# Recommendation kernel on one core: top and dense layers over batches of up to four tiles, wider product rounds and chunks, and all engine programs unrolled, GpSimd's with new waits

## The chip, the cores and the metric

The kernel runs on one core of one Trainium2 chip. The metric is the device time of one execution in microseconds, as the median over runs. Three runs of the kernel before gave 768.77, 771.14 and 771.28 us; the median is 771.14 us.

## What is computed

The reference, cut to what matters (B = 2048 samples, 26 fields of 12500 rows, D = 64, all float32):

```python
emb = emb_tables[jnp.arange(26)[:, None], x_cat]          # 26 gathered rows a sample
dense_embed = price[:, None] @ Wp + bp                     # (B, 64)
feats = concat([transpose(emb, (1, 0, 2)), dense_embed[:, None, :]], axis=1)   # (B, 27, 64)
gram = einsum('bid,bjd->bij', feats, feats)                # 27 x 27 products a sample
interactions = gram[:, IU, JU]                             # the 351 pairs above the diagonal
h = relu(dense_embed @ W1 + b1)                            # 64 -> 128
dense_out = relu(h @ W2 + b2)                              # 128 -> 64
t = relu(concat([interactions, dense_out], axis=1) @ Wt1 + bt1)   # 415 -> 256
out = (t @ Wt2 + bt2)[:, 0]
```

## The kernel before

**Tiles.** The batch is cut into 16 tiles of 128 samples. For a tile, GpSimd issues one indirect DMA for each of the 26 fields (line 191); each fetches 128 rows of 64 floats, one row a partition, into `gathered`. That makes 416 gathers. They are grouped in four chunks of fields, (0, 8), (8, 16), (16, 24) and (24, 26), with one semaphore a chunk.

**Transposes.** When a chunk has landed, TensorE transposes two fields at a time (line 383), with 64 dimensions of two fields on 128 partitions. ScalarE copies the odd fields and VectorE the even ones out of PSUM into `feats` (line 139; line 154 for the last tile, whose samples are laid out differently so that half of the tile can be multiplied before all fields are there).

**Products.** A group is four samples; one matmul of a group against itself gives the 4 x 4 blocks of products of which the diagonal ones are wanted (line 414). A tile has 16 groups in each of two partition halves. They are done in four rounds of 32 samples, in two alternating PSUM buffers of two banks. After each round both engines copy the wanted blocks into `gram`, eight copies of 32 x 56 elements an engine (line 129).

**Dense and top layers.** In each tile, the dense branch takes two matmuls (lines 389 and 393) with ReLUs on ScalarE (lines 236 and 240), and the top layer takes for each half m of its 256 outputs one matmul with `dense_out` (line 425) and seven with `gram` (line 432). ScalarE and VectorE apply the ReLU (lines 245 and 336), a last product with `Wt2` gives the scores (line 440), and ScalarE stores them (line 249). An fp32 matmul of the program stands in the trace as two matmuls and two weight loads; a transpose as one of each.

**Order.** Each engine has its own program, and semaphores alone tie them. Four of them have a hardware loop: GpSimd over all 16 tiles, TensorE and ScalarE over tiles 1 to 13, VectorE over tiles 0 to 13, with the remaining tiles written out. In GpSimd's loop each chunk begins with a wait on `tile_idx_set[c]` (line 188) and a no-operation (line 189). `tile_idx` holds the row numbers of one tile alone: ScalarE refills a chunk's part of it from `row_idx` (line 219) once that chunk of the tile before has been transposed. So both the single `gathered` buffer and `tile_idx` come free by the same event. The tiles' row numbers are computed at the start by VectorE.

**The last tile.** Tile 15 is written out on TensorE: transposes of chunk 0 and the top layer of tile 14, transposes of chunk 1, scores of tile 14, dense branch, product rounds 0 and 1, transposes of chunks 2 and 3, rounds 2 and 3, top layer, scores. For tiles 14 and 15 `keep_warm` puts unused matmuls of 256 columns at set places (line 372): `WARM` gives their number, (0, 12, 4, 1, 1) for tile 14 and (0, 7, 3, 1, 1) for tile 15. SyncE writes the result at the end (line 167).

Of the kernel before, what the change touches and what calls it, by code (L numbers as in the profile page):

```python
# [6 lines left out]
FIELDS, VOCAB, BATCH, D = 26, 12500, 2048, 64  # L7
# [11 lines left out]
ROUNDS = 4  # L19
# [8 lines left out]
NPAIR = SLOTS * (SLOTS - 1) // 2  # L28

# [6 lines left out]
def rec_kernel(nc, price, x_cat, table, consts, w1, w2, wt1_pairs, wt1_dense, out):  # L36
# [3 lines left out]
    with ExitStack() as ctx:  # L40
# [25 lines left out]
        dense = sb("dense", [D, P])  # L66
        hidden = sb("hidden", [BM1, P])
        dense_out = sb("dense_out", [BM2, P])
        top = sb("top", [P, 2 * P])
# [11 lines left out]
        ps_top = [ps_mlp[m][:, 0:P] for m in range(2)]  # L81
        ps_hidden = ps_mlp[0][:, P:2 * P]
        ps_dense_out = ps_mlp[0][0:BM2, 2 * P:3 * P]
        ps_score = ps_mlp[1][0:1, P:2 * P]
# [12 lines left out]
        tile_idx_set = [sem(f"tile_idx_set{c}") for c in range(len(CHUNKS))]  # L97
        chunk_gathered = [sem(f"chunk_gathered{c}") for c in range(len(CHUNKS))]
        chunk_transposed = [sem(f"chunk_transposed{c}") for c in range(len(CHUNKS))]
# [18 lines left out]
        NC = len(CHUNKS)  # L118

        gram_to = gram[:, :].rearrange("p (j h g s) -> p h g j s", j=SLABS, h=2, g=GROUPS, s=GROUP)  # L120
        gram_from = [ps[:, :].rearrange("p (h g s j c) -> p h g s j c", h=2, g=RG, s=GROUP, j=PAD // GROUP, c=GROUP)
                     for ps in ps_gram]

        def evacuate_gram(copy, r, quads):

            last = None
            for s in quads:
                for c in range(GROUP):
                    last = copy(gram_to[QUAD * c:QUAD * (c + 1), :, RG * r:RG * (r + 1), :, s],  # L129
                                gram_from[r % 2][QUAD * s:QUAD * (s + 1), :, :, s, 0:SLABS, c])  # L130
            return last

        def evacuate_chunk(copy, c, q):
# [3 lines left out]
            src = ps_trans[c % 2][:, 0:n * P].rearrange("p (k h b) -> p h b k", k=n, h=2)  # L137
# [4 lines left out]
        def evacuate_unit_chunk(copy, c, kk):  # L142

            f0, f1 = CHUNKS[c]
            src = ps_trans[c % 2][:, :].rearrange("p (m q h b) -> p m q h b", m=BANK // P, q=2, h=2)
# [14 lines left out]
        def _(sp):  # L160
# [5 lines left out]
            sp.wait_ge(score_stored, TILES + 1)  # L166
# [4 lines left out]
        def _(pool):  # L171
# [13 lines left out]
            with pool.Fori(0, TILES) as t:  # L185
                for c, (f0, f1) in enumerate(CHUNKS):

                    pool.wait_ge(tile_idx_set[c], t + 1)
                    pool.nop(nofuse=True)  # L189
                    for f in range(f0, f1):  # L190
                        pool.indirect_dma_start(out=gathered[:, f * D:(f + 1) * D], out_offset=None, in_=rows,  # L191
                                                in_offset=bass.IndirectOffsetOnAxis(ap=tile_idx[:, f:f + 1], axis=0))\
                            .then_inc(chunk_gathered[c], 16)

        @block.scalar
        def _(act):
# [7 lines left out]
            act.wait_ge(rows_made, 3)  # L204
            act.sem_inc(trans_evac_act, 2)
            act.sem_inc(gram_evac_act, 2)
            act.sem_inc(score_stored, 1)

            def dense_features(dst, part, first, n, t):

# [321 lines left out]
```

## Time and profile before

| What | Value |
|---|---|
| median of three runs | 771.14 us (768.77 to 771.28) |
| profiled execution: span from its first to its last instruction | 540.9 us |
| profiled execution: its own time | not recorded apart from the span |
| median of the runs less the span | 230.2 us |
| GpSimd busy | 393.8 us, 73% of the span |
| TensorE matmuls busy | 291.1 us, 54% |
| ScalarE busy | 246.8 us, 46% |
| VectorE busy | 190.2 us, 35% |
| mean granted clock of TensorE | 0.719 |
| mean DMA rate | 30 GB/s |

The profile lists what lies between the first and the last instruction of the program. What the device does before and after, which the runs' times include, is in no row of it. A busy share is time with an instruction of that engine under way; only waits that end on the chain that finishes last are worth anything.

### The profile page before, as it was taken

What the parts mean: (1) busy time and instruction counts of PE and PEld (TensorE: products, weight loads), DVE (VectorE), ACT (ScalarE), POOL (GpSimd) and SP (SyncE); (2) the same over time, 40 slices, a digit from 0 to 9 for tenths busy, and PEclk for the clock granted to TensorE, in tenths of its full rate; (3) what the DMA queues carried; (4) which work ended last, traced back from release to release, by engine and by line L of the source; (5) the groups of instructions that cost most, each with busy time, mean ns of one, the idle gap of its engine ahead of it and who ended that gap; (6) DMA issues with size and microseconds to landing.
All of it is one profiled execution on the core that took longest, in us unless ns stands there. A gap on an engine that the chain in (4) does not pass through costs nothing.

```text
span 540.9 us, 6578 instructions
## 1 busy us (share of the span) xinstructions
PE 291.1 (54%) x1932; PEld 234.6 (43%) x1932; DVE 190.2 (35%) x672; ACT 246.8 (46%) x816; POOL 393.8 (73%) x425
## 2 busy tenths in 40 slices
PE   0027465382744638466382644727275372786785
PEld 0017354271533517255271533616154261574564
DVE  3016043160613416053160612516043160612553
ACT  0127255271734527265281733637255281733653
POOL 6777777777777777777777777777777777777750
PEclk9997758576585856667567685767758586588888
DMA  6333332333333333333333333333332333332110
GB/s 186 27 26 30 25 27 26 27 26 26 26 27 26 27 26 27 25 26 26 26 27 26 27 27 25 27 26 27 26 26 26 27 26 26 26 26 26 29 23 1
DMA packets 14345, 16.07 MB, mean 30 GB/s; under 512 B 7169, under 2 KB 7425, under 8 KB 14209
## 3 DMA queue, kind: packets, MB, share of 16 engines
q0 software_dynamic: 13312, 13.66, 31.2%
q1 hardware_dynamic: 578, 2.19, 1.1%
q10 hardware_dynamic: 448, 0.14, 0.1%
q8 instruction: 4, 0.07, 0.0%
q14 instruction: 3, 0.02, 0.0%
HBM read 15.95 MB, written 0.01 MB: 29 GB/s over the span
## 4 chain that ended last, share of the span: by engine, by line
POOL 70%; issue 26%; PE 1%; ACT 1%; DMA 1%; POOLq 1%; DVE 0%
POOL gathered L191 70%; PE ps_mlp L432 1%; ACT gram L129 1%; DMA gathered<-in_table,tile_idx 1%; DMA raw_idx<-in_x_cat 0%; POOLq L185 0%; PE ps_gram L414 0%; POOLq L40 0%; POOLq L189 0%; PE ps_mlp L425 0%; PE ps_mlp L440 0%; DVE feats L154 0%; DVE top L336 0%; ACT scores L249 0%; PE ps_trans L383 0%
## 5 line engine op out<-in xcount | busy, mean ns | idle before, releaser
L191 POOL DMA_INDIRECT gathered<-in_table,tile_idx x416 | 392.7, 944 | 128.6 <-issue 126.5
L383 PE MATMUL ps_trans<-ident,gathered 128*128 128x128 f32 x208 | 50.1, 370 | 189.9 <-DMA gathered<-in_table,tile_idx 189.0
L129 ACT COPY gram<-ps_gram 32x56 f32<-32x56 f32 x512 | 131.1, 256 | 41.9 <-PE ps_gram L414 35.2
L129 DVE COPY gram<-ps_gram 32x56 f32<-32x56 f32 x512 | 130.1, 254 | 54.4 <-PE ps_gram L414 46.6
L414 PE MATMUL ps_gram<-feats 64*128 64x128 f32 x1024 | 112.8, 395 | 38.1 <-ACT feats L139 18.2
L414 PEld LDWEIGHTS ps_gram<-feats 64*128 64x128 f32 x1024 | 102.4, 295 | 49.2 <-DVE gram L129 25.5
L139 DVE COPY feats<-ps_trans 64x256 f32<-64x256 f32 (+1 forms) x120 | 45.3, 378 | 218.4 <-PE ps_trans L383 217.2
L383 PEld LDWEIGHTS ps_trans<-ident,gathered 128*128 128x128 f32 x208 | 30.5, 180 | 205.8 <-issue 148.3
L219 ACT CAST tile_idx<-row_idx 128x8 uint32 (+3 forms) x61 | 12.0, 196 | 203.3 <-PE ps_trans L383 202.7
L432 PE MATMUL ps_mlp<-gram,wt1p_sb 128*128 128x128 f32 x448 | 69.6, 317 | 18.1 <-ACT gram L129 14.9
L432 PEld LDWEIGHTS ps_mlp<-gram,wt1p_sb 128*128 128x128 f32 x448 | 63.4, 225 | 24.1 <-DVE gram L129 21.5
L139 ACT COPY feats<-ps_trans 64x256 f32<-64x256 f32 (+1 forms) x120 | 53.8, 448 | 2.1
L336 DVE TENSOR_SCALAR top<-ps_mlp,consts_sb 128x128 f32<-128x128 f32 x16 | 5.6, 351 | 66.4 <-PE ps_mlp L432 66.4
L425 PE MATMUL ps_mlp<-dense_out,wt1d_sb 64*128 64x128 f32 x64 | 19.0, 383 | 0.0
L372 PE MATMUL ps_trans<-wt1p_sb,ident 128*128 128x256 f32 x60 | 16.1, 416 | 0.0
L245 ACT ACTIVATE top<-ps_mlp,consts_sb 128x128 f32<-128x128 f32 x16 | 5.9, 367 | 21.7 <-PE ps_mlp L432 21.7
L211 ACT ACTIVATE feats<-price_bc,consts_sb 64x64 f32 (+1 forms) x32 | 15.6, 487 | 0.4
L425 PEld LDWEIGHTS ps_mlp<-dense_out,wt1d_sb 64*128 64x128 f32 x64 | 11.9, 232 | 6.4 <-issue 5.2
L372 PEld LDWEIGHTS ps_trans<-wt1p_sb,ident 128*128 128x128 f32 x60 | 11.8, 207 | 2.4 <-issue 0.3
L440 PE MATMUL ps_mlp<-top,consts_sb 128*1 128x128 f32 x64 | 11.6, 314 | 0.4 <-DVE top L336 0.4
L393 PE MATMUL ps_mlp<-hidden,w_sb 128*64 128x128 f32 x32 | 11.0, 447 | 1.1 <-ACT hidden L236 1.1
L389 PE MATMUL ps_mlp<-dense,w_sb 64*128 64x128 f32 x32 | 9.6, 388 | 0.0
(26 smaller groups left out, 56.6 us busy)
## 6 DMA issues: line engine op xcount, KB each, us to landing
gathered<-in_table,tile_idx POOLq DMA_INDIRECT x416, 3.3
price_bc<-in_price SPq DMA_DIRECT2D x1, 1024.0 KB, 5.7
wt1p_sb<-in_wt_pairs SPq DMA_DIRECT2D x1, 896.0 KB, 8.3
raw_idx<-in_x_cat SPq DMA_DIRECT2D x1, 195.0 KB, 3.2
w_sb<-in_w ACTq DMA_DIRECT2D x2, 32.0 KB, 5.4
wt1d_sb<-in_wt_dense ACTq DMA_DIRECT2D x1, 64.0 KB, 8.2
consts_sb<-in_consts ACTq DMA_DIRECT2D x1, 4.5 KB, 2.0
raw_idx<-in_x_cat SPq DMA_DIRECT2D x1, 13.0 KB, 1.8
```

The lines of the kernel that those rows point to most:

```text
L129: last = copy(gram_to[QUAD * c:QUAD * (c + 1), :, RG * r:RG * (r + 1), :, s], gram_from[r % 2][QUAD * s:QUAD * (s + 1), :, :, s, 0:SLABS, c])
L139: last = copy(feats[D * h:D * (h + 1), :, 1 + f0 + q:f1 + q:2], src[D * q:D * (q + 1), h, :, :])
L191: pool.indirect_dma_start(out=gathered[:, f * D:(f + 1) * D], out_offset=None, in_=rows, in_offset=bass.IndirectOffsetOnAxis(ap=tile_idx[: ...
L211: return nc.scalar.activation(dst, price_bc[part, bass.ds(t * P + first, n)], ACT.Identity, bias=const(BP, part), scale=const(WP, part))
L219: nc.scalar.copy(tile_idx[:, f0:f1], row_idx[:, bass.ds((t + 1) * FIELDS + f0, f1 - f0)])\
L372: nc.tensor.matmul(ps_trans[bank][:, 0:TM1], ident[:, :], wt1p_sb[:, 0:TM1], start=True, stop=True)
L383: last = nc.tensor.transpose(ps_trans[c % 2][:, k * P:(k + 1) * P], gathered[:, f * D:(f + 2) * D], ident[:, :])
L393: nc.tensor.matmul(ps_dense_out, w2_sb[:, :], hidden[:, :], start=True, stop=True)\
L414: last = nc.tensor.matmul(ps_gram[r % 2][:, h * BANK + g * P:h * BANK + (g + 1) * P], group, group, start=True, stop=True)
L425: nc.tensor.matmul(ps_top[m], wt1d_sb[:, m * P:(m + 1) * P], dense_out[:, :], start=True, stop=False)
L432: last = nc.tensor.matmul(ps_top[m], wt1p_sb[:, j * TM1 + m * P:j * TM1 + (m + 1) * P], gram[:, j * P:(j + 1) * P], start=False, stop=(j = ...
L440: last = nc.tensor.matmul(ps_score, const(WT2 + m), top[:, m * P:(m + 1) * P], start=(m == 0), stop=(m == 1))
```

## The change

It does the following.

- **Chunks.** Tiles 0 to 14 have two chunks of fields, (0, 14) and (14, 26), in place of four. Their transposes go to one PSUM buffer of two banks. The last tile keeps the four chunks of before, in two alternating banks, under names of its own (`LAST_CHUNKS`, `last_gathered`, `last_transposed`).
- **Rounds.** Tiles 0 to 14 have two product rounds of 64 samples in place of four of 32. A round fills all four banks, so the next round waits until both engines have copied. Copies are of 32 x 112 elements, eight an engine and round. The last tile keeps four rounds in alternating buffers.
- **Batches.** The dense and top layers, the score product and their ReLUs run once for a batch of tiles: tiles 0-3, 4-7, 8-11, 12-13, 14 and 15, over up to 512 columns. `gram` holds two batches. The top layer of a batch stands on TensorE behind the first transposes of the next batch's first tile, its scores behind the second transposes. Hidden layer, dense output, top layer and scores share two PSUM banks; the hidden layer of a batch now waits for `score_stored` of the batch before.
- **GpSimd.** The loop over tiles is gone: 416 gathers are written out. `gathered` has two buffers. Row numbers are read straight from `row_idx`, now integers; `tile_idx`, ScalarE's refills of it (line 219) and the no-operation are gone. New waits: at each chunk, that the same chunk of the tile before has landed; at chunk 0 of tile t, that chunk 1 of tile t-2 has been transposed; at chunk 1 of tile t, that chunk 0 of tile t-1 has been. 
- **Loops.** TensorE, ScalarE and VectorE are written out too.
- **Warming.** The unused matmuls of tile 14 are gone; those of tile 15 stay as they were.

The diff, cut to its core:

```diff
-ROUNDS = 4
+ROUNDS = 2
-CHUNKS = [(0, 8), (8, 16), (16, 24), (24, 26)]
-WARM = {TILES - 2: (0, 12, 4, 1, 1), TILES - 1: (0, 7, 3, 1, 1)}
+CHUNKS = [(0, 14), (14, 26)]
+LAST_CHUNKS = [(0, 8), (8, 16), (16, 24), (24, 26)]
+LAST_ROUNDS = 4
+BATCHES = [(0, 4), (4, 8), (8, 12), (12, 14), (14, 15), (15, 16)]
+WIDE = 4
+BUFFERS = 2
+WARM = (0, 7, 3, 1, 1)
...
-        row_idx = sb("row_idx", [P, (TILES + 1) * FIELDS])
-        tile_idx = sb("tile_idx", [P, FIELDS], u32)
-        gathered = sb("gathered", [P, FIELDS * D])
+        row_idx = sb("row_idx", [P, TILES * FIELDS], u32)
+        gathered = sb("gathered", [P, BUFFERS * ROW])
-        gram = sb("gram", [P, SLABS * P])
+        gram = sb("gram", [P, 2 * SLABS * WIDE * P])
-        ps_gram = [pb(f"ps_gram{i}", [P, 2 * BANK]) for i in range(2)]
-        ps_trans = [pb(f"ps_trans{i}", [P, BANK]) for i in range(2)]
+        ps_gram = pb("ps_gram", [P, 4 * BANK])
+        ps_trans = pb("ps_trans", [P, 2 * BANK])
...
-            with pool.Fori(0, TILES) as t:
+            def gather(t, f, done):
+                at, to = t * FIELDS + f, (t % BUFFERS) * FIELDS + f
+                pool.indirect_dma_start(out=gathered[:, to * D:(to + 1) * D], out_offset=None, in_=rows,
+                                        in_offset=bass.IndirectOffsetOnAxis(ap=row_idx[:, at:at + 1], axis=0))\
+                    .then_inc(done, 16)
+
+            for t in range(LAST):
+                if t == 0:
+                    pool.wait_ge(rows_made, 1)
+                else:
+                    pool.wait_ge(rows_made, 3)
                 for c, (f0, f1) in enumerate(CHUNKS):
-
-                    pool.wait_ge(tile_idx_set[c], t + 1)
-                    pool.nop(nofuse=True)
+                    if t > 0:
+                        pool.wait_ge(chunk_gathered[c], 16 * (f1 - f0) * t)
+
+                    if c == 0 and t > 1:
+                        pool.wait_ge(chunk_transposed[1], t - 1)
+                    if c == 1 and t > 0:
+                        pool.wait_ge(chunk_transposed[0], t)
                     for f in range(f0, f1):
-                        pool.indirect_dma_start(out=gathered[:, f * D:(f + 1) * D], out_offset=None, in_=rows,
-                                                in_offset=bass.IndirectOffsetOnAxis(ap=tile_idx[:, f:f + 1], axis=0))\
-                            .then_inc(chunk_gathered[c], 16)
+                        gather(t, f, chunk_gathered[c])
+
+            pool.wait_ge(chunk_transposed[1], LAST - 1)
+            for c, (f0, f1) in enumerate(LAST_CHUNKS):
+                if c == 2:
+                    pool.wait_ge(chunk_transposed[0], LAST)
+                for f in range(f0, f1):
+                    gather(LAST, f, last_gathered[c])
...
-                if next_indices:
-                    nc.scalar.copy(tile_idx[:, f0:f1], row_idx[:, bass.ds((t + 1) * FIELDS + f0, f1 - f0)])\
-                        .then_inc(tile_idx_set[c], 1)
...
+            def hidden_layer(n):
+                pe.wait_ge(dense_made, n + 1)
+                if n > 0:
+                    pe.wait_ge(score_stored, n)
+                nc.tensor.matmul(ps_mlp[0][:, 0:width(n)], w1_sb[:, :], dense[:, 0:width(n)], start=True, stop=True)\
+                    .then_inc(hidden_summed, 1)
...
+            for t in range(LAST):
+                n = batch_of[t]
+                first = t == BATCHES[n][0]
+                transpose_chunk(t, 0)
+                if first and n > 0:
+                    top_layer(n - 1)
                 transpose_chunk(t, 1)
+                if first and n > 0:
+                    score(n - 1)
+                gram_round(t, 0)
+                if first:
+                    hidden_layer(n)
+                gram_round(t, 1)
+                if first:
+                    dense_out_layer(n)
+
+            n = batch_of[LAST]
+            transpose_last(0)
+            top_layer(n - 1)
+            transpose_last(1)
+            score(n - 1)
+            hidden_layer(n)
+            dense_out_layer(n)
+            for r in range(LAST_ROUNDS // 2):
+                gram_last(r)
+            transpose_last(2)
+            transpose_last(3)
+            for r in range(LAST_ROUNDS // 2, LAST_ROUNDS):
+                gram_last(r)
+            top_layer(n)
+            score(n)
```

On ScalarE the last tile's order becomes: copies of chunk 0, dense features, ReLU of the top layer of tile 14, copies of chunk 1, scores of tile 14, ReLU of the hidden layer, ReLU of the dense output, rounds 0 and 1. Before, the hidden ReLU and the dense output's stood ahead of the scores.

## Rows read from the trace of the kernel before

**Rows 1.** The page: span, and the chain that ended last, by engine
```profile
span 540.9 us, 6578 instructions
...
POOL 70%; issue 26%; PE 1%; ACT 1%; DMA 1%; POOLq 1%; DVE 0%
```

**Rows 2.** The gathers' line, whole span: duration min/median/max, idle before, time to landing
```profile
L191 POOL DMA_INDIRECT gathered<-in_table,tile_idx x416: 940/944/1114, 4.3 to 522.5; - x139
...
  issue: 126.5, 415
...
DMA to landing us min/median/max: 2.3/3.3/5.5
```

**Rows 3.** Timeline of GpSimd: gathers 0, 1, 26 and 415 (start us, us, what)
```profile
4.30 1.11 POOL L191 DMA_INDIRECT gathered<-in_table,tile_idx  x1 [2.16 <-DVE tile_idx L308]
5.71 0.94 POOL L191 DMA_INDIRECT gathered<-in_table,tile_idx  x1 [0.30 <-issue]
...
36.92 0.94 POOL L191 DMA_INDIRECT gathered<-in_table,tile_idx  x1 [0.30 <-issue]
...
522.47 0.94 POOL L191 DMA_INDIRECT gathered<-in_table,tile_idx  x1 [0.31 <-issue]
```

**Rows 4.** Busy time of two stretches (us, then PE, PEld, DVE, ACT, POOL; clock; DMA)
```profile
497.60:506.20 8.60, 6.13 (x55) 4.74 (x52) 8.11 (x32) 8.18 (x32) 6.51 (x7) 0.80 0.21 30
484.00:490.00 6.00, 3.94 (x19) 3.13 (x17) 0.00 (x0) 0.00 (x0) 4.49 (x5) 1.00 0.41 28
```

**Rows 5.** The gathers' line in 497 to 506 us, then in 484 to 490 us
```profile
L191 POOL DMA_INDIRECT gathered<-in_table,tile_idx x8: 940/944/947, 496.3 to 505.0; - x8
...
L191 POOL DMA_INDIRECT gathered<-in_table,tile_idx x5: 940/944/945, 483.8 to 488.8; - x5
```

**Rows 6.** The chain of waits from 505 us: GpSimd's sequencer at the loop's exit
```profile
508.59 1.09 POOLq L40
```

**Rows 7.** Groups of instructions by shape: busy us, mean ns | idle before
```profile
L129 DVE COPY gram<-ps_gram 32x56 f32<-32x56 f32 x512 | 130.1, 254 | 54.4 <-PE ps_gram L414 46.6
...
L139 DVE COPY feats<-ps_trans 64x256 f32<-64x256 f32 x90 | 37.6, 418 | 201.6 <-PE ps_trans L383 200.5
...
L139 DVE COPY feats<-ps_trans 64x64 f32<-64x64 f32 x30 | 7.7, 258 | 16.9 <-PE ps_trans L383 16.7
```

**Rows 8.** Timeline of the last tile's end, TensorE and ScalarE
```profile
513.46 0.60 PE L440 MATMUL ps_mlp<-top,consts_sb 128*1 128x128 f32 x4
...
515.12 0.37 ACT L236 ACTIVATE hidden<-ps_mlp,consts_sb 128x128 f32<-128x128 f32 x1
...
516.15 3.28 PE L414 MATMUL ps_gram<-feats 64*128 64x128 f32 x32
...
519.36 3.29 PE L372 MATMUL ps_trans<-wt1p_sb,ident 128*128 128x256 f32 x14
...
522.73 0.66 PE L383 MATMUL ps_trans<-ident,gathered 128*128 128x128 f32 x4
...
525.28 0.33 PE L383 MATMUL ps_trans<-ident,gathered 128*128 128x128 f32 x1 [0.60 <-DMA gathered<-in_table,tile_idx]
...
526.30 2.06 PE L414 MATMUL ps_gram<-feats 64*128 64x128 f32 x32 [0.25 <-DVE feats L154]
...
532.11 3.06 PE L432 MATMUL ps_mlp<-gram,wt1p_sb 128*128 128x128 f32 x14 [2.94 <-ACT gram L129]
...
535.83 1.83 PE L432 MATMUL ps_mlp<-gram,wt1p_sb 128*128 128x128 f32 x14
```

**Rows 9.** Busy time and granted clock of two stretches, columns as in rows 4
```profile
516.00:519.40 3.40, 3.40 (x35) 3.12 (x33) 1.06 (x5) 1.68 (x7) 2.56 (x3) 0.60 0.20 26
...
532.00:535.10 3.10, 2.99 (x14) 2.80 (x14) 0.00 (x0) 0.00 (x0) 0.00 (x0) 0.56 0.00 0
```

**Rows 10.** The page: DMA queues of kind instruction (packets, MB, share)
```profile
q8 instruction: 4, 0.07, 0.0%
q14 instruction: 3, 0.02, 0.0%
```

More of the change, by code:

```diff
@@ L203, in _, with dense_features @@
             act.wait_ge(feats_zeroed, 1)
[L204 to L209, printed above, removed]
-                return nc.scalar.activation(dst, price_bc[part, bass.ds(t * P + first, n)], ACT.Identity,
+            def dense_features(dst, part, first, n):
+                return nc.scalar.activation(dst, price_bc[part, first:first + n], ACT.Identity,
@@ L266, in _ @@
-            odd_fields(0, 0)
-            tile(0, first=True)
-            with act.Fori(1, TILES - 2) as t:
-                tile(t)
-            tile(TILES - 2, next_evacuate=evacuate_unit_chunk)
-            t = TILES - 1
-            dense_parts(t)
-            odd_fields(1, t, False, evacuate_unit_chunk)
-            hidden_relu(t)
-            dense_out_relu(t)
-            store_scores(t - 1)
-            for r in range(ROUNDS // 2):
+                evacuate_gram(nc.scalar.copy, t, r, (2, 3)).then_inc(gram_evac_act, 1)
@@ L342, in tile, with top_relu @@
+            def top_relu(n):
+                dve.wait_ge(top_summed[1], n + 1)
+                nc.vector.tensor_scalar(top[1][:, 0:width(n)], ps_mlp[1][:, 0:width(n)], const(BT1 + 1), 0.0,
+                                        ALU.add, ALU.max).then_inc(top_made, 1)
+            for t in range(LAST):
+                n = batch_of[t]
+                even_fields(0, t)
+                if t == BATCHES[n][0] and n > 0:
+                    top_relu(n - 1)
+                even_fields(1, t)
                 for r in range(ROUNDS):
@@ L343, in tile @@
                     gram_round(r, t)
[L344 to L354 removed]
+            t, n = LAST, batch_of[LAST]
+            even_last(0)
+            top_relu(n - 1)
+            even_last(1)
@@ new lines, in wait_trans_evac, with wait_gram_evac, transpose_fields @@
+            def wait_trans_evac(n):
+                if n > 0:
+                    pe.wait_ge(trans_evac_dve, n)
+                    pe.wait_ge(trans_evac_act, n)
+            def wait_gram_evac(n):
+                if n > 0:
+                    pe.wait_ge(gram_evac_dve, n)
+                    pe.wait_ge(gram_evac_act, n)
+            def transpose_fields(t, f0, f1, to):
+                base = (t % BUFFERS) * ROW
+                for k in range((f1 - f0) // 2):
+                    f = f0 + 2 * k
+                    last = nc.tensor.transpose(ps_trans[:, to + k * P:to + (k + 1) * P],
+                                               gathered[:, base + f * D:base + (f + 2) * D], ident[:, :])
+                return last
@@ new lines, in dense_out_layer, with gram_matmuls @@
+            def dense_out_layer(n):
+                pe.wait_ge(hidden_made, n + 1)
+                nc.tensor.matmul(ps_mlp[1][0:BM2, 0:width(n)], w2_sb[:, :], hidden[:, 0:width(n)], start=True, stop=True)\
+                    .then_inc(dense_out_summed, 1)
+            def gram_matmuls(first, groups, to, apart):
+                for g in range(groups):
+                    for h in range(2):
+                        at = (first + g) * GROUP
+                        group = feats[D * h:D * (h + 1), at:at + GROUP, :].rearrange("p s j -> p (s j)")
+                        out_at = to + h * apart + g * P
+                        last = nc.tensor.matmul(ps_gram[:, out_at:out_at + P], group, group, start=True, stop=True)
+                return last
@@ L473, in _ @@
-            score(t)
+            for t in range(LAST):
+                n = batch_of[t]
+                first = t == BATCHES[n][0]
+                transpose_chunk(t, 0)
+                if first and n > 0:
+                    top_layer(n - 1)
+                transpose_chunk(t, 1)
+                if first and n > 0:
+                    score(n - 1)
+                gram_round(t, 0)
+                if first:
+                    hidden_layer(n)
+                gram_round(t, 1)
+                if first:
+                    dense_out_layer(n)
```

304 lines of the change are left out of this document (136 added, 168 removed).

## Prediction

> **What bounds the kernel now.** I read the page's chain that ended last first, because it says whose time is the span. It names GpSimd for 70% and "issue" for 26%, every other engine for about 1% [rows 1]. Then the gathers' line: 416 of them, 0.944 us each with hardly any spread, and ahead of 415 of them an idle of 126.5 us in all, 0.305 us apiece, put down to "issue", that is, to nothing that the profile shows [rows 2]. The timeline confirms it: gather 1 starts at 5.71 us and gather 415 at 522.47 us, so the spacing is 516.76 / 414 = 1.248 us. Gather 26 is the first of tile 1, behind a pass of the loop, a wait and the no-operation, and has the same 0.30 us ahead of it as any other [rows 3]. So GpSimd never waits for another engine once it has begun. The span is: start until gather 0 at 4.30 us, the gathers until the last one's start at 522.47 us, and a tail of 540.9 - 522.5 = 18.4 us, in which the last fields land and the last tile is finished [rows 1, 3].
>
> Two further views say why the loop costs nothing. In the chain, GpSimd's sequencer is at the loop's exit at 508.59 us and done at 509.68 us, 12.8 us before the last gather starts [rows 6]: it runs some ten gathers ahead of the work. And where VectorE is busy 8.11 of 8.60 us the gathers take 940/944/947 ns, where it is idle 940/944/945 ns [rows 4, 5].
>
> The runs' median is 771.14 us, 230.2 us more than the profiled span; the profiled execution has no time of its own beside its span. These 230.2 us are in no row. I carry them over unchanged, and the doubt on them goes into the rivals.
>
> **The change, part by part.**
>
> GpSimd's program. 416 gathers stay, of the same shape: 128 rows of 64 floats by a column of 128 row numbers. Removed: 16 passes of the loop, 64 waits and 64 no-operations. They cost nothing now, because the sequencer does them about ten gathers ahead [rows 3, 6]. The spacing is bounded by 1.248 us (nothing changes) and 0.944 us (all "issue" gone, -126.5 us); the 0.305 us stand ahead of gathers with no wait, no loop and no no-operation between them as well as at the tile's border, so I take 1.248 us.
>
> The new waits. "Same chunk of the tile before has landed": at chunk 0 the last gather waited for started 13 gathers before, 16.2 us, against a landing of 3.3 us, at most 5.5 us [rows 2, 3]. At chunk 1 it is 15 gathers. While the sequencer waits, about ten gathers are queued. Cost 0. What stands behind such a wait on GpSimd is all later gathers, so these waits matter if they ever bite.
>
> The gates on the transposes. The nearest to biting is chunk 0 of tile t behind chunk 1 of tile t-2, where t-2 is first of a batch, since the wide top layer stands on TensorE ahead of that transpose. Its price: 14 matmuls of 128 columns took 1.83 us at full clock and 3.06 us at a granted clock of 0.56 [rows 8, 9]. For 512 columns I take between four times the one and four times the other, 7.3 to 12.2 us, twice for both halves, plus the products with `dense_out` at a seventh of that: 17 to 28 us. Chunk 1 lands 12 x 1.248 = 15.0 us behind chunk 0, so its transposes come 2 to 13 us late. The gate is looked at for a gather that starts 27 x 1.248 = 33.7 us after chunk 1's last gather, of which landing takes 3.3 us: 30 us of room against 13 us. Cost 0; the cover is gone only if the wide top layer takes over 45 us. At chunk 1 of tile t the gate asks for chunk 0 of tile t-1, which stands ahead of the top layer: no danger.
>
> TensorE, ScalarE and VectorE, tiles 0 to 14. Per tile two rounds of 32 matmuls, 2.06 to 3.28 us each [rows 8], each followed by eight copies of 112 elements. A copy of 56 took 254 ns, and 192 more elements a partition cost 418 - 258 = 160 ns on VectorE [rows 7], so I take 300 ns, between 254 (free) and 508 (double). A round is then 2.4 us of copies and a tile's rounds, no longer overlapped, 2 x (3.3 + 2.4) = 11.4 us at most, 15 us with the upper copy. With transposes and a quarter of a wide top layer it is under 30 us of a tile's 26 x 1.248 = 32.4 us. All of this gets cheaper for ScalarE and VectorE (fewer, larger copies, no refills) and hides behind the gathers before and after: worth 0.
>
> The start. One addition over 26 columns stands where four over 8, 8, 8 and 2 stood, and gather 0 waits for it and not for the first alone: some hundredths of a microsecond, and the no-operation is gone. 0.
>
> The tail. From the last landing on the program is the same: one transpose, 32 product matmuls, copies, 28 top matmuls, scores. What differs is what stands ahead. The hidden layer of tile 15 now waits for `score_stored` of tile 14. The score product ends at 514.1 us, but ScalarE stores scores behind the copies of chunk 1, which hold it until 515.1 us (the hidden ReLU started right then, at 515.12 [rows 8]). So scores are stored at about 515.5, the hidden matmuls run until 516.0, their ReLU until 516.5, the dense output's until 517.2, and rounds 0 and 1 start at 517.2 us where they started at 516.15: 1.0 us later. Behind them on TensorE stand 14 warming matmuls, which ended at 522.65, just ahead of the transposes of chunk 2 at 522.73 [rows 8]. These now start at 523.65. Then 0.66 us of transposes and six warming matmuls, 6/14 x 3.29 = 1.41 us, and chunk 3 can be transposed at 525.72 where it was at 525.28: **+0.4 us**. The lower end is -1.2 us, if the first 14 top matmuls meet full clock (3.06 down to 1.83). The upper end is +3.0 us: 0.4 and 1.2 for the products of rounds 2 and 3 (2.06 up to 3.28) and 1.2 for the second 14 top matmuls, with the remaining small ones in the rest. I take +0.4, since tile 15's order and its warming are unchanged.
>
> **Sum.** Span 540.9 + 0.4 = 541.3 us; with the 230.2 us outside, 771.5 us. A measurement of this kernel can tell about 0.3%, 2.3 us, from no change.
>
> **Rivals.**
>
> *Slower, the longer program.* Place: what is fetched and set up before the first gather, which no row shows, and the instruction queues. The trace has seven packets of 0.09 MB for them [rows 10]. By the code TensorE, ScalarE, VectorE and GpSimd hold about 1,400 instructions before (a quarter of what they execute) and 4,200 after, so 0.27 MB would move, 0.18 MB more. If that stands ahead of the work, at the gathers' rate of 26 to 28 GB/s, it is 7 us, **778 us**; the lower end is 0, if it is fetched beside the work. It decides from 2.3 us on, a third of it uncovered. For it: 230.2 us outside the span are unexplained. Against it: no engine in the span shows a stall for its instructions. 15%. The Trainium skill, Runtime: NRT & Kernel Launch, section Instruction fetch mechanics, says that a sequencer fetches the next block while it executes the present one, so that a long program is mostly hidden, and that a taken branch outside the fetched window stalls. By it the longer program costs nothing inside the span, which would leave the 771.5 us, and the trace agrees as far as the loop goes: 0.30 us at its border as elsewhere.
>
> *Slower, the clock in the tail.* The part before the last tile is less dense on TensorE (the warming of tile 14 is gone, the top layer is one block in four tiles). If all of the tail's matmuls run at the lower clock, it is the upper end, +3.0 us: **774.1 us**. For it: the clock was 0.60 in rounds 0 and 1 and 0.56 after the copies [rows 9]. Against it: tile 15's own warming is kept. 8%.
>
> *Slower, a gate that bites.* Four first tiles of batches with, say, 10 us each of stalled gathers. The room of 17 us above speaks against it: 3%, about 811 us.
>
> *Faster, the loop costs something where it is not profiled.* If the sequencer were not ahead in the timed runs, each of 16 passes would show what the exit took, 1.09 us [rows 6], and writing it out would give 17 us: **754 us**. The profiled execution shows the reverse, but cannot account for 230.2 us. 10%.
>
> *Faster, less contention.* If gathers were slowed by VectorE's traffic, halving its copies would shorten them; the most that the rows leave is 944 - 940 ns for 416 of them, 1.7 us: 769.8 us. Equal medians with VectorE busy and idle speak against it. 2%, counted as faster. The Trainium skill, GPSIMD Engine Reference, section Specifications, says that GpSimd shares its SBUF interfaces with VectorE and contends with some of its instructions. This trace shows no sign of it for these copies.
>
> **How the numbers follow.** The forecast case has 62%, of which 56 fall within 0.3% and 3 on either side, for the scatter of runs (768.77 to 771.28). Slower: 3 + 15 + 8 + 3 = 29%. Faster: 3 + 10 + 2 = 15%. Range: from 767 us, the lowest run less the tail's 1.2 and a little scatter, to 779 us, the longer program's 778 and scatter. It leaves out the unprofiled loop and the biting gate, 13%, and some edges.
>
> **What would show it.** In the changed kernel's profile: gathers at 0.94 us with 0.30 us ahead of each, first start near 4.3 and last near 522.5 us; no wait of GpSimd on TensorE; the wide top layer 17 to 28 us and its tile's second transposes late by 2 to 13 us; rounds 0 and 1 of tile 15 about 1 us later, the last transpose at 525.7; a span of 541.3 us. I am wrong if the spacing of gathers moves, if gathers wait for transposes, or if median and span no longer stand 230 us apart: the last would say that the program's length or its loops cost time that the profile doesn't cover.

## The result and the profile after

The kernel after took 675.37 us (median of four runs, 673.98 to 683.1), beside 769.95 us for the kernel before in the same session: a ratio of 0.8795 with a 95% interval of 0.8748 to 0.8842, 12% faster. I had predicted 771.5 us and no change.

The first thing to read is that in each of these runs the recorded span is 1.8 us short of the time: 673.98 us stand beside a span of 672.2 us. In every timed execution of this study that has both, whatever the kernel, they are 1.75 to 2.11 us apart. The 230.2 us "outside the span" of the prediction therefore never lay outside. They were the difference between two conditions in which a chip can be. The trace with a span of 540.9 us [rows 1] was of the one, the 771 us of the other. I call them **quiet** (the kernel before takes 543 to 544 us) and **disturbed** (763 to 770 us). Of the chips used below, 2, 3, 6 and 9 were quiet. Chip 14 was disturbed, in both series of runs made on it, and is the only such chip here; which chips the runs of this section used is not on record. For reading a change, each condition needs a trace of its own.

The page of the kernel after, taken in the disturbed condition (span; busy time of each engine; the chain that ended last, by engine; the instruction queues):

```profile
span 672.2 us, 4362 instructions
...
PE 256.0 (38%) x1496; PEld 180.9 (27%) x1496; DVE 145.4 (22%) x358; ACT 169.1 (25%) x405; POOL 393.8 (59%) x425
...
q8 instruction: 12, 0.20, 0.1%
...
q14 instruction: 10, 0.08, 0.0%
...
another core or an unknown queue 51%; issue 15%; DVE 13%; PE 13%; ACT 7%; DMA 0%; SPq 0%; ACTq 0%
```

No engine is busy for 60% of the span, GpSimd has left the chain [rows 1 had it at 70%], and half of it is put down to "another core or an unknown queue" in a program on one core. That name, "remote" in other views, is given to a wait that no recent event in the trace explains. The gathers' line and the longest waits of the same kernel (us in total, times, longest):

```profile
L200 POOL DMA_INDIRECT gathered<-in_table,row_idx x416: 938/944/1112, 3.7 to 623.7; - x139
...
  issue: 121.3, 398
  PE ps_trans L421: 97.8, 15
...
  remote: 9.3, 2
```

```profile
DVE gram L141 <- remote: 330.0, 24, 55.2
ACT gram L141 <- remote: 324.9, 24, 55.3
...
POOL gathered L200 <- PE ps_trans L421: 97.8, 15, 20.6
```

Duration and issue gap of a gather are those of [rows 2]; new are 107.1 us (97.8 and the 9.3 under "remote") in which GpSimd stands still for transposes, about once a tile. The timeline of the kernel after shows what is late (start us, us, what, idle before it):

```profile
41.43 3.79 PE L458 MATMUL ps_gram<-feats 64*128 64x128 f32 x32 [1.30 <-issue]
...
45.00 1.52 PE L443 MATMUL ps_mlp<-dense,w_sb 64*128 64x512 f32 x2
...
96.53 3.17 ACT L141 COPY gram<-ps_gram 32x112 f32<-32x112 f32 x8 [55.34 <-remote]
...
99.95 3.79 PE L458 MATMUL ps_gram<-feats 64*128 64x128 f32 x32 [53.43 <-ACT gram L141]
...
106.59 0.94 POOL L200 DMA_INDIRECT gathered<-in_table,row_idx  x1 [20.62 <-PE ps_trans L421]
```

The product round ends at 45.22 us, and the copies that read it start at 96.53 us, 51 us later. Nothing else held ScalarE or VectorE. The semaphore events kept in the trace say that it is the signal that is late and not the copies: the increment behind this round stands at 96.51 us, and at 45.25 us, 0.03 us behind the round's last matmul, in the quiet trace of the same kernel that is read further down. The windows view tells when they were let go (window, length, then for PE, PEld, DVE, ACT and POOL the busy time with its instructions, granted clock, DMA share, GB/s):

```profile
46.50:86.00 39.50, 0.02 (x1) 0.00 (x0) 0.00 (x0) 0.00 (x0) 30.03 (x32) 0.54 0.33 27
86.00:96.50 10.50, 0.00 (x0) 0.00 (x0) 0.00 (x0) 0.00 (x0) 0.00 (x0) 0.50 0.04 3
96.50:106.00 9.50, 5.87 (x41) 4.55 (x41) 5.23 (x14) 5.94 (x15) 0.00 (x0) 0.60 0.00 0
```

For 39.5 us GpSimd gathers, and the other engines stand still with finished products in PSUM. Then the gate stops GpSimd, and 10.5 us into that pause everything goes on at once.

### The profile page after: what moved, and what is told of

Read it like the earlier page. It is cut to its first block, busy times and chain, and to the rows that moved or that the text cites. A ratio compares the mean times of both kernels' runs of the same rounds, so it can differ in the third digit from the quotient of the medians.

```text
span 672.2 us, 4362 instructions
## 1 busy us (share of the span) xinstructions
PE 256.0 (38%) x1496; PEld 180.9 (27%) x1496; DVE 145.4 (22%) x358; ACT 169.1 (25%) x405; POOL 393.8 (59%) x425
## 4 chain that ended last, share of the span: by engine, by line
another core or an unknown queue 51%; issue 15%; DVE 13%; PE 13%; ACT 7%; DMA 0%; SPq 0%; ACTq 0%
DVE gram L141 9%; PE ps_mlp L489 8%; ACT gram L141 5%; DVE feats L151 3%; PE ps_gram L458 2%; ACT feats L151 1%; PE ps_trans L421 1%; PE ps_trans L404 1%; PE ps_mlp L481 1%; DVE top L370 0%; ACT feats L239 0%; DMA raw_idx<-in_x_cat 0%; DVE feats L352 0%; ACT feats L166 0%
## 5 line engine op out<-in xcount | busy, mean ns | idle before, releaser
L200 POOL DMA_INDIRECT gathered<-in_table,row_idx x416 | 392.6, 944 | 229.9 <-issue 121.3
L141 ACT COPY gram<-ps_gram 32x112 f32<-32x112 f32 (+1 forms) x272 | 97.1, 357 | 395.5 <-remote 324.9
L141 DVE COPY gram<-ps_gram 32x112 f32<-32x112 f32 (+1 forms) x272 | 96.6, 355 | 404.3 <-remote 330.0
L489 PE MATMUL ps_mlp<-gram,wt1p_sb 128*128 128x512 f32 (+2 forms) x168 | 63.0, 538 | 7.5 <-DVE gram L141 4.2
L151 DVE COPY feats<-ps_trans 64x448 f32<-64x448 f32 (+1 forms) x60 | 36.7, 612 | 50.4 <-issue 40.8
L151 ACT COPY feats<-ps_trans 64x448 f32<-64x448 f32 (+1 forms) x60 | 34.1, 569 | 44.3 <-PE ps_trans L421 24.1
L489 PEld LDWEIGHTS ps_mlp<-gram,wt1p_sb 128*128 128x128 f32 x168 | 33.6, 234 | 39.2 <-issue 24.7
L239 ACT ACTIVATE feats<-price_bc,consts_sb 64x64 f32<-64x64 f32 x32 | 15.7, 490 | 0.7
L481 PE MATMUL ps_mlp<-dense_out,wt1d_sb 64*128 64x512 f32 (+2 forms) x24 | 13.5, 655 | 4.0 <-ACT dense_out L271 2.6
L404 PE MATMUL ps_trans<-wt1p_sb,ident 128*128 128x256 f32 x24 | 6.1, 391 | 0.0
```

The lines of the kernel that those rows point to most:

```text
L141: last = copy(gram_to[QUAD * c:QUAD * (c + 1), n % 2, t - BATCHES[n][0], :, rg * r:rg * (r + 1), :, s], source[QUAD * s:QUAD * (s + 1), :, ...
L151: last = copy(feats[D * h:D * (h + 1), :, 1 + f0 + q:f1 + q:2], src[D * q:D * (q + 1), h, :, :])
L200: pool.indirect_dma_start(out=gathered[:, to * D:(to + 1) * D], out_offset=None, in_=rows, in_offset=bass.IndirectOffsetOnAxis(ap=row_idx[ ...
L239: return nc.scalar.activation(dst, price_bc[part, first:first + n], ACT.Identity, bias=const(BP, part), scale=const(WP, part))
L404: nc.tensor.matmul(ps_trans[:, BANK * bank:BANK * bank + TM1], ident[:, :], wt1p_sb[:, 0:TM1], start=True, stop=True)
L481: nc.tensor.matmul(ps_mlp[m][:, 0:w], wt1d_sb[:, m * P:(m + 1) * P], dense_out[:, 0:w], start=True, stop=False)
```

## The experiments

The working theory, R in what follows: in the disturbed condition, **while gathers stream, what TensorE has finished is made known to the other engines only slowly, and the lag is worked off when the gathers pause.** In the expectations, A1 is the form of it in which the gates' pauses help, and A2 the rival in which they are pure loss. C is a second rival, without any lag: the chain of transposes, copies and products itself is slow, and instructions beside it are free.

**The kernel before, unchanged** (chip 14). 

> The kernel before, unchanged, to see what a profiled execution of it looks like beside its timed ones. Theory A (the execution whose trace was shown first was an unusual one; the timed ones contain stalls such as the changed kernel's trace shows, in which products are done and the copies that wait for them start tens of us later): span about 768 us, GpSimd's gathers interrupted by waits of some 230 us in all. Theory B (230 us lie outside the span of every execution): span 541 us again and a time of 770 us.

764.42 us, ratio 1.0002; profiled span 761.8 us. This is the trace that the prediction should have had:

```profile
span 761.8 us, 6578 instructions
```

```profile
L191 POOL DMA_INDIRECT gathered<-in_table,tile_idx x416: 938/944/1479, 4.3 to 726.0; - x139
...
  ACT tile_idx L219: 206.2, 15
  issue: 123.5, 400
```

```profile
41.07 3.79 PE L414 MATMUL ps_gram<-feats 64*128 64x128 f32 x32 [1.10 <-issue]
...
76.03 8.86 ACT L129 COPY gram<-ps_gram 32x56 f32<-32x56 f32 x32 [35.27 <-remote]
...
85.88 0.94 POOL L191 DMA_INDIRECT gathered<-in_table,tile_idx  x1 [16.47 <-ACT tile_idx L219]
```

GpSimd stands still for 206.2 us, in 15 of 16 tiles. The account of the 89.6 us between the two spans: pauses 206.2 - 107.1 = 99.1 us less, issue gaps 2.2 less, start 0.6 less, which puts the last gather 102 us earlier; the tail behind it grows from 35.8 to 48.5 us, 12.7 more.

**Without gates** (chip 14).

```diff
-BUFFERS = 2
+BUFFERS = 16
-                    if c == 0 and t > 1:
-                        pool.wait_ge(chunk_transposed[1], t - 1)
-                    if c == 1 and t > 0:
-                        pool.wait_ge(chunk_transposed[0], t)
```

> The changed kernel with 16 buffers for the gathered rows and no wait of GpSimd on transposes. Theory A1 (the stalls end when the gates stop the gathers, so the stream of gathers itself holds up the semaphores of TensorE): gathers without a pause until about 523 us, one long stall of TensorE until then, and after it the work of up to 15 tiles at about 20 us each, 750 to 850 us. Theory A2 (the stalls have another cause and the gates only hand them on to GpSimd): gathers end at 523 us, TensorE is at most one stall behind, 545 to 600 us.

873.84 us, 1.1455 (1.1348 to 1.1563): the slowest of all, and above the 750 to 850 us of A1. The gathers run through without a pause, 3.8 to 557.3 us, and the span is 868.5 us. Its gathers' line, and stretches of its timeline:

```profile
L200 POOL DMA_INDIRECT gathered<-in_table,row_idx x416: 940/947/1799, 3.8 to 557.3; - x139
```

```profile
118.80 3.14 ACT L141 COPY gram<-ps_gram 32x112 f32<-32x112 f32 x8 [77.54 <-remote]
...
122.19 3.75 PE L451 MATMUL ps_gram<-feats 64*128 64x128 f32 x31 [75.22 <-issue]
...
139.78 0.37 PE L414 MATMUL ps_trans<-ident,gathered 128*128 128x128 f32 x1 [2.43 <-issue]
...
141.18 0.18 PEld L414 LDWEIGHTS ps_trans<-ident,gathered 128*128 128x128 f32 x1 [2.62 <-issue]
...
142.58 0.37 PE L414 MATMUL ps_trans<-ident,gathered 128*128 128x128 f32 x1 [2.43 <-issue]
...
143.98 0.18 PEld L414 LDWEIGHTS ps_trans<-ident,gathered 128*128 128x128 f32 x1 [2.62 <-issue]
...
435.20 3.06 DVE L141 COPY gram<-ps_gram 32x112 f32<-32x112 f32 x8 [86.47 <-remote]
...
454.80 1.28 DVE L151 COPY feats<-ps_trans 64x448 f32<-64x448 f32 x2 [16.54 <-remote]
...
471.60 1.21 DVE L151 COPY feats<-ps_trans 64x384 f32<-64x384 f32 x2 [15.52 <-remote]
...
561.20 3.13 DVE L141 COPY gram<-ps_gram 32x112 f32<-32x112 f32 x8 [88.39 <-remote]
```

Weight loads and matmuls alternate at exactly 1.40 us, with nothing that they wait for. The last four lines show the same beat in the signals. VectorE's copies start 19.6, 16.8 and 89.6 us apart, which is 14, 12 and 64 times 1.40 us, and 14, 12 and 64 are the numbers of TensorE instructions between them: seven transposes, six transposes and a product round, with their weight loads. So while gathers stream, the lag is counted in instructions, one per 1.40 us, and not in the time that they take.

In the other direction nothing is slow here: ScalarE's copies end at 121.94 us and TensorE starts its round at 122.19. A2 falls. Without pauses TensorE does, at 1.40 us each, some 395 instructions in the 553 us of the gathers (the trace has 408 started by then), two tiles of 16 and a part of the third, and the rest afterwards, in 311 us.

The gathers themselves also take longer in places, which neither form expected: they end at 557.3 us and not at 523, and GpSimd is busy 427.5 us against 393.8. From 220 us on, 163 of them follow each other at 1.40 us as well. What the two have in common is not shown.

**One part alone** (chip 14): only GpSimd written out, with direct row numbers and the gate on the transposes in place of ScalarE's refill; then only the other three loops written out.

```diff
-            with pool.Fori(0, TILES) as t:
+            for t in range(TILES):
-                    pool.wait_ge(tile_idx_set[c], t + 1)
-                    pool.nop(nofuse=True)
+                    pool.wait_ge(rows_made, 1 if t == 0 else 3)
+                    if t > 0:
+                        pool.wait_ge(chunk_transposed[c], t)
```

> The kernel before with GpSimd's program alone written out: row numbers read from row_idx, at each chunk one wait that the same chunk of the tile before has been transposed, no refills by ScalarE. If GpSimd's loop or its refilled row numbers cost the time (the rival in which the loop costs something in the timed runs): 545 to 680 us. If the chunks, rounds and batches did it: 770 us as before.

```diff
-            with act.Fori(1, TILES - 2) as t:
+            for t in range(1, TILES - 2):
-            with dve.Fori(0, TILES - 2) as t:
+            for t in range(0, TILES - 2):
-            with pe.Fori(1, TILES - 2) as t:
+            for t in range(1, TILES - 2):
```

> The kernel before with the loops of TensorE, ScalarE and VectorE written out and GpSimd's loop kept. If waits against register values and loop passes on these three engines cost the time: 545 to 680 us. If a longer program costs time: over 775 us. If neither: 770 us.

GpSimd's part: 716.06 us from two runs 2.6% apart (706.72, 725.4), so 38 to 57 us less than the 763.49 us beside it, with no interval; in the trace of the 725.4 us run GpSimd's pauses are 169.5 us, for 206.2. It takes away a loop and a hop over ScalarE, whose refill stands behind that engine's other work; which of the two counts was not separated. The three loops: 747.53 us, 0.9799 (0.9677 to 0.9922), a gain that may be under 1%. Both times lie between the values expected, so neither part alone is the whole cause. A program written out is not slower, against the rival of the longer program.

**More for TensorE, fewer passes for TensorE, more pauses.** Each was run on a quiet and on the disturbed chip. The first expectation of each pair had the disturbed condition in mind and met quiet chip 6, where it doesn't apply.

```diff
+                for _ in range(32):
+                    nc.tensor.transpose(ps_trans[:, 2 * BANK - P:2 * BANK], ident[:, :], ident[:, :])
                 gram_round(t, 1)
```

> The changed kernel with 32 unused transposes of the identity more on TensorE in each of tiles 0 to 14, between the two product rounds (64 matmuls and weight loads a tile, about 2 us of TensorE, which is busy 38%). Theory R (while gathers stream, TensorE gets rid of finished instructions, and with them of its semaphore increments, at only one in about 1.4 us; only in pauses of the gathers does it catch up, at some 16 in a microsecond by 187 instructions a tile and 10 us lost a tile): 64 more cost about 4 us a tile, 675 + 60 = 735 us. Theory C (the chain of transposes, copies, products and copies is what is late, and instructions beside it are free): at most 2 us a tile on that chain, 675 to 705 us.

> The changed kernel with 32 unused transposes more on TensorE in each of tiles 0 to 14. Where the kernel before takes 544 us they cost nothing (542.9 us). Theory R where it takes 765 us: about 4 us a tile, 735 us, a ratio of 0.96. Theory C: 675 to 690 us, a ratio of 0.88 to 0.90.

```diff
-        feats = sb("feats", [P, HALF, PAD])
+        feats = sb("feats", [P, HALF, PAD], mybir.dt.bfloat16)
```

> The changed kernel with feats held in bfloat16, so that a product is one matmul and one weight load in place of two and two: 64 instructions a tile fewer on TensorE. The products are rounded to bfloat16 inputs. Theory R: about 4 us a tile less, 675 - 60 = 615 us. Theory C: products take half of 3.8 us a round, 7 us a tile less of a chain that waits for nothing else, 570 us if that chain set the time, or no change if the stalls are of another kind.

> The changed kernel with feats in bfloat16, 64 instructions a tile fewer on TensorE, inputs of the products rounded. Where the kernel before takes 544 us it changes nothing (543.6 us). Theory R where it takes 765 us: about 615 us, a ratio of 0.80. If the number of instructions on TensorE doesn't matter: 675 us, 0.88.

```diff
                     for f in range(f0, f1):
                         gather(t, f, chunk_gathered[c])
+                    pool.wait_ge(chunk_gathered[c], 16 * (f1 - f0) * (t + 1))
```

> The changed kernel with GpSimd waiting behind each chunk until that chunk's gathers have landed, a pause of about 3 us every 14 gathers or 12. Theory R: the pauses let TensorE catch up and replace most of the pauses that the gates force now, so 650 to 700 us. Theory C or any in which gathers don't disturb TensorE: the pauses add up, 29 x 3 = 87 us, 740 to 765 us.

> The changed kernel with GpSimd waiting behind each chunk until its gathers have landed. On a chip where the kernel before takes 544 us this took 613 us, 71 us more, by 31 pauses. Theory R on a chip where it takes 765 us: the pauses let TensorE's finished instructions go and take the place of the gates' pauses, 640 to 700 us, a ratio of 0.84 to 0.92 to before. Theory C: they add to the changed kernel's 675 us, 745 us, a ratio of 0.97.

| Kernel | quiet chips 3, 6 | ratio | chip 14 | ratio |
|---|---|---|---|---|
| before | 543.27, 543.99 | | 764.83 | |
| after | 542.15 | 0.998 | not run; 0.8795 x 764.83 = 672.7 | 0.8795 |
| 960 more TensorE instructions | 543.63 | 0.9992 | 718.88 | 0.9399 (0.9353 to 0.9444) |
| bf16 products | 544.77 | 1.001 | 652.0 | 0.8524 (0.85 to 0.8549) |
| pause after each chunk | 613.57 | 1.129 | 641.35 | 0.8385 (0.8289 to 0.8481) |

The row of the kernel after is from chip 3, the other three of the quiet column from chip 6. The gathers' line of the three on chip 14, in this order, with the waits ahead of them:

```profile
L201 POOL DMA_INDIRECT gathered<-in_table,row_idx x416: 938/944/1252, 3.7 to 663.8; - x139
...
  PE ps_trans L422: 140.7, 15
```

```profile
L200 POOL DMA_INDIRECT gathered<-in_table,row_idx x416: 942/947/1302, 3.7 to 600.8; - x139
...
  remote: 66.0, 13
...
  PE ps_trans L421: 16.8, 5
```

```profile
L200 POOL DMA_INDIRECT gathered<-in_table,row_idx x416: 938/944/1112, 3.7 to 593.3; - x139
...
  DMA gathered<-in_table,row_idx: 77.9, 29
```

On a quiet chip, TensorE's instructions are free. On the disturbed one 960 more cost 46 us, 0.048 us each, and show as longer pauses of GpSimd (146.7 us in all, for 107.1). Theory R had forecast 735 us, 16 too high; rival C, 675 to 690. But C was priced with 2 us a tile of TensorE's own work, and the trace has more. This line is 27 of one tile's 32 extra transposes:

```profile
156.88 3.96 PE L515 MATMUL ps_trans<-ident 128*128 128x128 f32 x27
```

At that rate 32 take 4.7 us, 70 us in 15 tiles, and the extra transposes hold 5.5% of the chain that ended last, 39 us. So this run doesn't separate the number of instructions from the time they take; what shows that the number counts is the beat in the run without gates. With bf16, products take half as many instructions (TensorE's 2,992 matmuls and loads become 1,968), and 21 us go, 0.020 us each. At 0.048 us each it would be 49, and 615 us were expected: here the direction is right and the size is not.

Short pauses of GpSimd's own (77.9 us in 29 of them) replace the gates' and leave only 2.7 us of those: 31 us faster than after, inside the 640 to 700 us expected. The same pauses cost 71 us where no lag has to be worked off. This last version beats both kernels on the disturbed chip and loses 13% on a quiet one, so it is no replacement.

The kernel after itself and the two variants once more on quiet chip 3:

> The changed kernel, unchanged, beside the kernel before on the same chip. Theory R (two conditions of a chip: one in which TensorE's finished instructions are held up while gathers stream, and one in which they are not): where the kernel before takes 765 us, 670 to 680 us; where it takes 544 us, 544 us too, ratio 1.00, because the gathers' 519 us bound both. A theory in which the change itself does 12% would give a ratio of 0.88 in either.

> The changed kernel with 32 unused transposes more on TensorE in each of tiles 0 to 14. Theory R: where the kernel before takes 765 us, 64 more instructions a tile cost some 4 us a tile, about 735 us against 675 us for the changed kernel; where it takes 544 us, nothing, 544 us. Theory C (a chain of work): 675 to 705 us in the first condition.

> The changed kernel with feats held in bfloat16: products of one matmul and one weight load in place of two and two, 64 instructions a tile fewer, with inputs rounded to bfloat16. Theory R: about 615 us where the kernel before takes 765 us, 544 us where it takes 544 us.

542.15 us (ten runs), 0.998 (0.9962 to 0.9998); 542.91 and 543.64 us, within 0.13% of before. In the quiet condition the change is worth 0.2%, inside what I had called no change.

**Gathers of two tiles only** (chip 6), the rest of the work kept.

```diff
-            for t in range(LAST):
+            for t in range(BUFFERS):
```

> The changed kernel with only the first two tiles' rows gathered (14 of 16 tiles' gathers left out; all the other work runs on those rows). Theory R: once the two tiles' gathers are over no stall is seen and a tile takes about 20 us, 340 to 420 us in all. Theory C (the work itself stalls, gathers or not): 600 to 675 us.

387.42 us, 0.7129: without the other gathers (the scores are then those of the first two tiles' rows and not the reference's), the work of the other engines takes 387.42 / 16 = 24 us a tile, under the 32.4 us of a tile's gathers. That is why nothing done to them shows on a quiet chip. On the lag it says nothing, since a quiet chip has none.

**What the remaining chips left open.** Four runs were meant for a disturbed chip and met quiet ones (9, 9, 9 and 2): 32 one-element copies more a tile on VectorE and on ScalarE; the kernel before with all four loops written out, twice; pauses and bf16 together.

> The changed kernel with 32 unused copies of one element more on VectorE and 32 on ScalarE in each of tiles 0 to 14, 64 instructions a tile as in e12, behind the copies of the products. Where the kernel before takes 544 us: 544 us. Where it takes 765 us, if only TensorE's instructions are held up: 675 to 685 us, a ratio of 0.88 to 0.90. If every engine's are, or if what counts is the number of instructions of all engines: about 719 us as in e12, 0.94.

> The kernel before with all four loops written out and GpSimd waiting on transposes directly, but with its four chunks, four rounds and a top layer for every tile: the unrolling half of the change without the half that saves instructions on TensorE (54 of 241 a tile). Where the kernel before takes 544 us: 544 us. Where it takes 765 us: e2 gave 0.94 and e3 0.98 of it, so 700 to 716 us, 0.92 to 0.94; the rest to the changed kernel's 0.88 is then the fewer instructions, at e12's 44 us for 960 of them some 40 us.

> The kernel before with all four loops written out and GpSimd waiting on transposes directly, its chunks, rounds and layers as they were. On a chip where the kernel before takes 543 us this took 542 us. Where it takes 765 us: 700 to 716 us, a ratio of 0.92 to 0.94, so that about half of the 12% is the writing out and the other half the fewer instructions.

> The changed kernel with the pauses of e11 and feats in bfloat16 (inputs of the products rounded). Where the kernel before takes 544 us: 613 us, as with the pauses alone. Where it takes 765 us: the pauses alone end the gathers at 593 us with 49 us behind them; with 64 instructions a tile fewer the backlog in the last tile shrinks, 615 to 635 us, a ratio of 0.80 to 0.83.

542.42 us (0.998), 542.1 (0.9978), 542.12 (0.9989) and 615.16 us (1.1325, as the pauses alone). They say that, on a quiet chip, small instructions and loops are worth some 0.2% or nothing. Whether ScalarE's and VectorE's instructions count on a disturbed chip stays open, and so does the exact split of the 12%.

## Why the prediction was wrong

**The step that failed** is the one in the first part: "These 230.2 us are in no row. I carry them over unchanged". A gap of 230.2 us between a span and a median was taken as a constant that lies around the program. It was a second condition of the chip inside the span, of which I had no row, and all that the change gained was made there. The list of what would prove me wrong named it ("if median and span no longer stand 230 us apart"); the forecast gave it 15% on the slower side, for 7 us, and 10% on the faster, for 17 us. With a gap of 30% of the time unexplained, the range of 767 to 779 us was not supportable.

**In the condition that was traced, the steps stand.** The unchanged kernel after on quiet chip 3, page and gathers' line:

```profile
span 542.0 us, 4362 instructions
...
POOL 62%; issue 22%; DMA 7%; PE 6%; ACT 2%; DVE 0%; POOLq 0%
```

```profile
L200 POOL DMA_INDIRECT gathered<-in_table,row_idx x416: 940/945/1112, 3.7 to 522.1; - x139
...
  issue: 122.2, 401
...
  DMA gathered<-in_table,row_idx: 4.3, 14
```

- GpSimd: spacing (522.1 - 3.7) / 415 = 1.249 us, predicted 1.248. It never waits for a transpose. The 14 waits on its own landings, 4.3 us, are the usual 0.30 us each under another name. The first gather came 0.6 us earlier, where I had put 0.
- Span: 542.0 us, predicted 541.3. That single trace lies 1.1 us above the one of before; the medians on chip 3 have the kernel after 1.1 us below. The +0.4 us is thus inside the scatter and not confirmed.

Its timeline, around the first wide top layer and in the tail:

```profile
153.46 1.73 PE L421 MATMUL ps_trans<-ident,gathered 128*128 128x128 f32 x7 [4.22 <-DMA gathered<-in_table,row_idx]
...
157.12 8.89 PE L489 MATMUL ps_mlp<-gram,wt1p_sb 128*128 128x512 f32 x14
...
166.99 6.28 PE L489 MATMUL ps_mlp<-gram,wt1p_sb 128*128 128x512 f32 x14
...
173.10 0.82 PE L421 MATMUL ps_trans<-ident,gathered 128*128 128x128 f32 x6
...
518.65 2.06 PE L458 MATMUL ps_gram<-feats 64*128 64x128 f32 x32
...
525.50 0.27 PE L421 MATMUL ps_trans<-ident,gathered 128*128 128x128 f32 x1
...
532.20 3.33 PE L489 MATMUL ps_mlp<-gram,wt1p_sb 128*128 128x128 f32 x14 [2.87 <-ACT gram L141]
...
536.18 2.63 PE L489 MATMUL ps_mlp<-gram,wt1p_sb 128*128 128x128 f32 x14
```

- The wide top layer: 155.12 to 173.27 us, 18 us, predicted 17 to 28. Second transposes 19.6 us behind the first, 4.6 us later than their 15.0; predicted 2 to 13.
- The tail: rounds 0 and 1 of tile 15 at 518.65 us (predicted 517.2; 516.15 before), the last transpose at 525.50 (predicted 525.72). The second top block took 2.63 us where it was 1.83 [rows 8]: a part of the clock rival came true, inside its 3.0 us.
- Copies of 112 elements were mis-sized, 371 ns for my 300, and hidden:

```profile
L141 DVE COPY gram<-ps_gram 32x112 f32<-32x112 f32 x240 | 89.1, 371 | 108.0 <-PE ps_gram L458 105.2
```

**Terms put at zero that carried the gain where the lag exists.** The prediction had "GpSimd never waits for another engine once it has begun" and "worth 0" for the work of the others. On the disturbed chip GpSimd's pauses go from 206.2 to 107.1 us. TensorE goes from 3,864 instructions (matmuls and loads) to 2,992, from 241 to 187 a tile. By estimate, 54 x 16 = 864 fewer are worth 41 us at the 0.048 us of the experiment with more of them, and 17 us at the 0.020 us of bf16. GpSimd's part was worth 38 to 57 us, the other loops' 2% or 16 us, these two measured alone. With 41, 48 and 16 us, 764 us become 659; with 17, 48 and 16 us, 683; measured, scaled to this chip, is 673. So the parts are of the right size together, and their split, or whether they overlap, is not shown.

**The rivals.** *The loop costs something where it is not profiled* (754 us, 10%) had the direction and, by luck, a part of the place: GpSimd's loop with its hop over ScalarE was 38 to 57 us of a gain of 92. Its mechanism, 1.09 us more at each pass of the loop, is not seen: also on chip 14 the issue gaps of the kernel before are 123.5 / 400 = 0.31 us, and its pauses are waits for ScalarE's refill. *The longer program* (778 us, 15%) is refuted: its 22 packets and 0.28 MB are what I had worked out (0.27), and the loops written out alone made nothing slower (0.9799 on chip 14, 0.9978 and 0.9989 on quiet chips). The Trainium skill, Runtime: NRT & Kernel Launch, section Instruction fetch mechanics, was right in this: mostly hidden. *The biting gate* (811 us, 3%) did bite, 107.1 us of it, with the opposite sign: by the run without gates it is these pauses that let TensorE go on. *Less contention*: the gathers still took 944 ns.

## What to carry to other kernels

When the time of the runs and the profiled span disagree by more than a few microseconds, suspect that the profile is of an execution unlike the one to be forecast: get a trace in the condition of the runs before costing a single edit, and until then let the range cover what the unexplained part could do. Waits named "remote" in a one-core program, behind a producer that ended tens of microseconds before, were here a late signal and not a slow producer. There, less work for TensorE and short pauses in the stream of gathers paid (21 and 31 us), while in the quiet condition the first paid nothing and the second cost its length.

## What was not expected of the hardware

The same kernel takes 543 us on four chips and 764 us on another, with gathers of the same 944 ns. On the latter, while gathers stream, TensorE's instructions appear one per 1.40 us, and the engines that copy products idle for 35 to 88 us; within some 10 us of a pause everything flows again. By the pauses, the backlog goes at about (187 - 23) x 15 / 107.1 = 23 instructions a microsecond, an estimate with the 32.4 us of a tile's gathers at 1.40 us each as the 23 that got through meanwhile. It is not the clock: TensorE's mean granted clock was 0.665 to 0.701 in the runs of the kernel after of 674 to 676 us, and 0.665 to 0.706 in its quiet runs of 540.5 to 544.1 us. What puts a chip into this condition is not known. That the recording of the profile has a part in it is an open rival, since every execution timed here was a recorded one.
